# A relational message pass with one head's share on GpSimd and the one-hot tiles on VectorE

## The reference, cut to what matters

```python
# relational layer, after the attention weights alpha (one for each edge and head) are known
xl_e = xl[src, edge_type]                                   # (E, 4 heads * 128)
msg = (xl_e.reshape(E, H, C) * alpha[..., None]).reshape(E, HC)
agg = jax.ops.segment_sum(msg, seg, num_segments=N * R).reshape(N, R, H, C)
h_rel = agg.mean(axis=2) + bias                             # mean over the 4 heads
h_msg = jnp.einsum('r,nrc->nc', gw, h_rel)                  # weighted sum over the 4 relations
h1 = _layernorm(h + h_msg, g1, bt1)                         # and so on: feed-forward, layer norm
```

## Time and profile before

| | us |
|---|---|
| median of 3 runs | 8074.86 (8072.14 to 8080.34) |
| profiled execution | 8083.27 |
| span of its trace | 8081.4 |
| `rel_sum`'s lots in it, from 6104 to 6871 us | 767 |

### The profile page before, as it was taken

One profiled execution on the slowest core, in us unless ns is written; L12 is line 12 of the kernel. 1 busy time (PEld: TensorE's weight loads), 2 busy tenths in 40 slices (PEclk: granted clock), 3 DMA queues, 4 the chain that ended last, 5 costly groups with the idle time before them and its releaser, 6 DMA issues. The chain is left out here.

```text
span 8081.4 us, 86320 instructions
## 1 busy us (share of the span) xinstructions
PE 4591.5 (57%) x20103; PEld 3072.2 (38%) x20222; DVE 4954.4 (61%) x18680; ACT 1892.6 (23%) x4901; POOL 5452.5 (67%) x5731
## 2 busy tenths in 40 slices
PE   3343452444443444459788888878884566433343
PEld 3333332444433444434333333333334556333333
DVE  4333362444453444477688888888888998533334
ACT  0000031222222222231023323222235665400001
POOL 7777717777737777712277777777765777577775
PEclk6555565555565555579899999999998999655555
DMA  2111113333322333338899999999986887111111
GB/s 73 51 51 51 51 25 83 78 78 77 77 61 71 77 79 78 74 134 336 307 347 348 349 349 346 345 348 344 346 311 222 281 279 253 35 51 51 51 51 52
DMA packets 572435, 1348.04 MB, mean 167 GB/s; under 512 B 101141, under 2 KB 138997, under 8 KB 558761
## 3 DMA queue, kind: packets, MB, share of 16 engines
q0 software_dynamic: 228864, 628.13, 26.0%
q1 hardware_dynamic: 328604, 689.76, 24.1%
q10 hardware_dynamic: 14476, 24.62, 1.0%
HBM read 1003.21 MB, written 338.89 MB: 166 GB/s over the span
## 5 line engine op out<-in xcount | busy, mean ns | idle before, releaser
L942 POOL DMA_INDIRECT gat_ring<-gat_table,psrc_idx x1664 | 1643.5, 988 | 777.3 <-issue 498.2
L578 DVE TENSOR_TENSOR acc<-acc,bank 128x129 f32 (+1 forms) x1664 | 480.2, 289 | 1250.1 <-PE bank L541 1205.4
L1931 POOL DMA_INDIRECT pair<-right_table,idx_r_idx x782 | 788.5, 1008 | 365.8 <-issue 212.8
L510 POOL DMA_INDIRECT gcn_sum_ring<-gcn_table,src_idx x782 | 769.8, 984 | 275.2 <-issue 238.0
L1931 POOL DMA_INDIRECT acc<-left_table,idx_l_idx x782 | 789.9, 1010 | 238.7 <-issue 208.1
L510 POOL DMA_INDIRECT gin_sum_ring<-in_x,src_idx x782 | 781.2, 999 | 250.7 <-issue 237.1
L2006 ACT ACTIVATE positive<-positive 128x512 f32<-128x512 f32 x782 | 492.2, 630 | 1588.9 <-DVE positive L2036 1588.9
L1984 PE MATMUL bank<-pair,ident 128*128 128x512 f32 x1564 | 832.7, 615 | 1.3 <-issue 0.7
L1006 PE MATMUL bank<-gat_ring,gat_hot 128*128 128x130 f32 x3328 | 719.8, 392 | 118.1 <-DVE gat_hot L1126 116.1
L541 PE MATMUL bank<-gcn_sum_ring,gcn_sum_hot 128*128 x1664 | 417.8, 431 | 619.1 <-DMA gcn_sum_ring<-gcn_table,src_idx 586.4
L541 PE MATMUL bank<-gin_sum_ring,gin_sum_hot 128*128 x1664 | 405.2, 420 | 569.7 <-DMA gin_sum_ring<-in_x,src_idx 534.2
(11 more groups left out here) (521 smaller groups left out, 8770.9 us busy)
## 6 DMA issues: line engine op xcount, KB each, us to landing
kept<-acc SPq DMA_DIRECT2D x391, 512.0 KB, 6.1
x_rows<-kept SPq DMA_DIRECT2D x195, 1024.0 KB, 5.3
gat_place<-local_rows SPq DMA_DIRECT2D x128, 416.0 KB, 3.9
left_table<-rel_out SPq DMA_DIRECT2D x49, 1032.0 KB, 5.0
right_table<-rel_out SPq DMA_DIRECT2D x49, 1032.0 KB, 3.9
feat<-attr_rows SPq DMA_DIRECT2D x194, 256.0 KB, 7.9
gat_ring<-gat_table,psrc_idx POOLq DMA_INDIRECT x1664
types<-type_rows SPq DMA_DIRECT2D x98, 256.0 KB, 6.1
```

Of the source, the lines that this page charges most:

```text
L510: e.indirect_dma_start(ring[:, at:at + F], None, table[:, :], bass.IndirectOffsetOnAxis(ap=ed["src"][:, i:i + 1], axis=0)).then_inc(*got[b ...
L942: e.indirect_dma_start(ring[:, at:at + TROW], None, table[:, :], bass.IndirectOffsetOnAxis(ap=ed["psrc"][:, i:i + 1], axis=0)).then_inc(*g ...
L1931: e.indirect_dma_start(to[j % NG][:, n * LROW:(n + 1) * LROW], None, tab[:, :], bass.IndirectOffsetOnAxis(ap=idx[:, i:i + 1], axis=0)).the ...
```

## The change

GpSimd no longer makes one-hot tiles. For each lot it makes the product of head 2 and the weights, for the lot's four tiles in one instruction of 128 x 512, into `temper` (the tile `soft_far`, one buffer), and adds that to the four tiles' halves j = 1 with a second instruction of 128 x 512, once ScalarE has signalled `scaled`. It signals `pooled` (a semaphore whose name in the listings is `summed`; `tempered` is `relued`). VectorE keeps head 0, so 4 products for a lot where there were 8, and makes the one-hot tiles of the lot in one comparison of 128 x 512. The node numbers for it are copied once into a PSUM bank. SyncE's loads, ScalarE's copy of a new group's weights and TensorE's matmuls wait for `pooled` as well as for `mixed`. ScalarE's work is the same.

```diff
             @block.gpsimd
             def _(e):
-                e.wait_ge(*placed.at(1))
-                for i in range(LOTS):
-                    if i >= NH:
-                        e.wait_ge(*product.at(i - NH + 1))
-                    for n in range(Q):
-                        m = e.tensor_scalar(hot[i % NH][:, n * P:(n + 1) * P], c["node_iota"][:, :],
-                                            ed["local"][:, i * Q + n:i * Q + n + 1], None, ALU.is_equal)
-                    m.then_inc(*hot_made.up())
+                for b in range(FULL):
+                    g, where = group_of(b * Q)
+                    if where == 0 or b == 0:
+                        e.wait_ge(*placed.at(g + 1))
+                    e.wait_ge(*kept_in[b % NR].at(b // NR + 1, 16))
+                    if b:
+                        e.wait_ge(*pooled.at(b))
+                    n = size(b)
+                    e.tensor_tensor(temper[:, 0:n, :], lot_of(b)[:, 0:n, 2 * F:3 * F],
+                                    weights_of(b, 2).to_broadcast([P, n, F]), ALU.mult).then_inc(*tempered.up())
+                    e.wait_ge(*scaled.at(b + 1))
+                    e.wait_ge(*tempered.at(b + 1))
+                    into = parts_of(b, 1)
+                    e.tensor_tensor(into, into, temper[:, 0:n, :], ALU.add).then_inc(*pooled.up())
...
             def _(e):
                 for b in range(FULL):
                     if b >= NR:
                         e.wait_ge(*mixed.at(b - NR + 1))
+                        e.wait_ge(*pooled.at(b - NR + 1))
...
                         if g:
                             e.wait_ge(*mixed.at(b - TURN // Q))
+                            e.wait_ge(*pooled.at(b - TURN // Q))
                         put(g + 1)
...
                     e.wait_ge(*hot_made.at(b + 1))
                     e.wait_ge(*mixed.at(min(b + 1, FULL)))
+                    e.wait_ge(*pooled.at(min(b + 1, FULL)))
...
                 e.wait_ge(*placed.at(1))
+                e.tensor_copy(iota, c["node_iota"][:, :]).then_inc(*iota_laid.up())
+                e.wait_ge(*iota_laid.at(1))
...
                     if i < LOTS:
-                        g, where = group_of(i * Q)
-                        if where == FIX and g + 1 < SGROUPS:
-                            soft.mend_group_vector(e, g + 1, fixed)
+                        if i >= NH:
+                            e.wait_ge(*product.at(i - NH + 1))
+                        e.tensor_tensor(
+                            hot[i % NH][:, 0:Q * P].rearrange("p (t n) -> p t n", n=P),
+                            iota.unsqueeze(1).to_broadcast([P, Q, P]),
+                            over(ed["local"][:, i * Q:(i + 1) * Q], P), ALU.is_equal).then_inc(*hot_made.up())
                     if i < FULL:
...
                         for t_ in range(i * Q, i * Q + size(i)):
-                            for j in range(2):
-                                h = 2 * j
-                                m = e.scalar_tensor_tensor(
-                                    out=part_of(t_, j), in0=row_of(t_)[:, h * F:(h + 1) * F], scalar=weight_of(t_, h),
-                                    in1=part_of(t_, j), op0=ALU.mult, op1=ALU.add)
+                            m = e.scalar_tensor_tensor(
+                                out=part_of(t_, 0), in0=row_of(t_)[:, 0:F], scalar=weight_of(t_, 0),
+                                in1=part_of(t_, 0), op0=ALU.mult, op1=ALU.add)
                         m.then_inc(*mixed.up())
```

More of the change, by code:

```diff
@@ L2071, in rel_sum @@
             "hot_made", "scaled", "mixed", "product", "added", "fixed", "turned", "placed")
+        pooled, tempered = k.begin("summed", "relued")
+        temper = soft.far[:, 0:Q * F].rearrange("p (n f) -> p n f", f=F)
         filled, brow_made, chained, x_back = k.begin("filled", "biased", "dve", "x_loaded")
+        iota, (iota_laid,) = k.psum[BANK_V][:, 0:P], k.begin("carried")
         LAST = SCHUNKS - 1
@@ L2078, in rel_sum, with weights_of @@
         part_of = lambda i, j: weighted[:, (i % RT * 2 + j) * F:(i % RT * 2 + j + 1) * F]
+        lot_of = lambda b: x_rows[:, b % NR * Q * LROW:(b % NR + 1) * Q * LROW].rearrange("p (n f) -> p n f", f=LROW)
+        parts_of = lambda b, j: weighted[:, b * Q % RT * 2 * F:(b * Q % RT + size(b)) * 2 * F].rearrange(
+            "p (n j f) -> p n j f", j=2, f=F)[:, :, j, :]
+        def weights_of(b, h):
+            g, m = group_of(b * Q)
+            n, m = divmod(m, SPAN)
+            return weight[g % 2][:, :].rearrange("p (j q) -> p j q", q=P)[:, 0:size(b), n * 32 + h * NRUN + m // RUN].unsqueeze(2)
         def weight_of(i, h):
@@ L2108, in _ @@
                 e.wait_ge(*mixed.at(FULL))
+                e.wait_ge(*pooled.at(FULL))
                 e.dma_start(x_rows[:, :], x_kept[:, :]).then_inc(*x_back.up(16))
@@ L2138, in _ @@
                     for i in range(b * Q, b * Q + size(b)):
-                        for j in range(2):
-                            h = 2 * j + 1
+                        for j, h in enumerate((1, 3)):
                             m = e.mul(part_of(i, j), row_of(i)[:, h * F:(h + 1) * F], weight_of(i, h))
@@ L2188, in _ @@
                 e.wait_ge(*placed.at(1))
+                e.tensor_copy(iota, c["node_iota"][:, :]).then_inc(*iota_laid.up())
+                e.wait_ge(*iota_laid.at(1))
                 for i in range(LOTS + 1):
+                    g, where = group_of(i * Q)
+                    if i < LOTS and where == FIX and g + 1 < SGROUPS:
+                        soft.mend_group_vector(e, g + 1, fixed)
                     if i < LOTS:
-                        g, where = group_of(i * Q)
-                        if where == FIX and g + 1 < SGROUPS:
-                            soft.mend_group_vector(e, g + 1, fixed)
+                        if i >= NH:
[4 more added lines that the diff above has]
+                            over(ed["local"][:, i * Q:(i + 1) * Q], P), ALU.is_equal).then_inc(*hot_made.up())
                     if i < FULL:
```

## The result

The changed kernel takes 8104.06 us (median of 7 runs, 8092.09 to 8110.16) against 8072.14 (7 runs, 8060.33 to 8080.34): ratio 1.0038, 95% interval 1.0026 to 1.0049. It is slower by 0.4%, 32 us where 66 had been forecast against the same median (63 against the traces). The profiled execution took 8107.66 us, its span 8105.8. The time lies inside the stated range, the sign is right, and the size is half of what was said.

What follows compares the result with a forecast made beforehand. VectorE was taken to bind the stage, level with the load ring; lots going from 3.755 to 4.1 us gave +68 us, the last 12 lots -5, so +63 on the median 8074.9: 8138 us, range 8010 to 8215.

Steps and rivals of the forecast that it cites:

- What bounds the stage: In `rel_sum`, VectorE's own work (3 x 3.40 us) binds, level with the ring of three loads (10.2 us).
- the loop of two lots: Landing, GpSimd's product of lot b+3, VectorE's remaining products of lot b+2: (5.4 + 1.3 + 1.1) / 2 = 3.9 us a lot.
- the ring: Experiments' rival: lots are longer because of the loads' ring of three and the added waits for `pooled`; no chance given.
- The hold: VectorE's products with two SBUF inputs are blocked while GpSimd runs a 128 x 512 instruction: 1.0 us a lot.
- Mending and unevenness: In the lots, mending of scores adds 0.15 us as before and about 0.05 for meeting GpSimd; late loads add nothing.
- The last 12 lots: After the last products, VectorE's 1.84 us a lot replaces 2.3: 24.5 us instead of 29.2, -5 us.
- Gained or lost in the span, one for one: Engines leave the stage together, so what the lots gain or lose passes fully into the whole span.
- Cover holds: Rival: the block is short or falls in VectorE's additions and comparison; 3.35 us a lot, -84 us, 7991 us; chance 0.24.
- Both instructions hit: Rival: GpSimd's addition and next product both hold VectorE's products, 1.4 us on average; 4.48 a lot, +137 us, 8212; chance 0.17.
- the times above keep the two apart: Argument against two holds in a lot: by the calculated times GpSimd's addition and next product don't both meet VectorE's products.

Runs made afterwards that it cites:

- e1: Changed kernel with GpSimd's product and addition cut from 128 x 512 to 128 x 8, all waits kept; ratio 0.9861 to the kernel before, 3.27 us a lot.
- e2: Changed kernel with ScalarE writing head 1 into PSUM, so VectorE's products have one SBUF input; ratio 0.9896 to the kernel before, 3.43 us a lot.
- e3: Changed kernel with one more wait: GpSimd's product starts only after VectorE mixed the lot before; ratio 0.9979 to the kernel before, 3.77 us a lot.
- e4: Kernel before with VectorE's one-hot comparison alone, its eight products kept, GpSimd idle in the stage; ratio 1.0054 to the kernel before, 4.06 us a lot.
- e8: e2 with VectorE's comparison made one lot earlier; ratio 0.9905 to the kernel before, last 12 lots 25.2 us.
- e7: The kernel before, unchanged, traced once more; 3.733 us a lot, stage 760.8 us, rest of the span 7318.9 us.
- e13: Changed kernel plus one GpSimd comparison with a per-partition number into a spare tile; single run 8123.6 us, beside 8072.9 for the kernel before.
- e6: Changed kernel with GpSimd's addition cut to 128 x 8, its product kept at 128 x 512; ratio 0.9963 to the kernel before, 3.74 us a lot.
- e5: Changed kernel with GpSimd's product cut to 128 x 8, the full-size addition adding the half to itself; ratio 0.9943 to the kernel before, 3.58 us a lot.

## Why the prediction was half right

**What bounds the stage, and the form of the loop: right.** VectorE stays the bound, and the loop of two lots (landing, GpSimd's product of lot b+3, the rest of VectorE's products of lot b+2) is in the rows after. e1, e2 and e3 leave no room for the ring alone.

**The hold: right in kind, 0.82 instead of 1.0 us.** Two lengths were taken too large. GpSimd's product over the strided rows took 1.06 and 1.10 us in the median with either group of weights, not the 1.27 of the earlier trace rows; the addition did take 1.27. And the comparison advances VectorE by 0.60 us, not 0.68, as e4 isolates. By start-to-start steps the sum is 1.16 + 0.60 + 1.05 + 0.82 = 3.63, and the rows show 3.63 to 3.69 where 3.9 was said. That the mean over all lots is 0.83 too is in part luck: it is made of lots with no hold, with one and with two.

**Mending and unevenness: too small.** Mending's own hold is 0.09 us a lot, not 0.05, and 0.1 us is left over for late loads and changes of group, where I had added nothing. With 3.66, 0.15, 0.09 and 0.1 the lot is 4.00. The errors cancel in part: 4.00 for 4.1, which is 48 us for 68.

**The last 12 lots: wrong, -0.3 instead of -5 us.** I let VectorE's 1.84 us bind (12 lots at 0.46 less give 23.7 us, not the 24.5 of the sum). The comparison of a lot stands behind the additions of the lot before last, so TensorE gets its one-hot tiles too late and the two take turns. The chain of waits of those rows was not followed in the prediction; e8 confirms it with 25.2 us.

**"Gained or lost in the span, one for one": the step that failed.** Stage +47.4 us (by e7's trace of before 51.7), whole +32 by the medians. So 15 to 20 us, by the two traces of before 23 and 26, came back in layers that the diff doesn't touch. The stretches of gathers account for 13 us of it, 25.6 saved in the first two layers and 12.6 given back in the third and the last; one comparison more undoes this in e13. The rest stays open. No row of before could have shown that GpSimd's comparisons touch them. With the stage's true +47 alone the forecast would have been high by a third; this term, put at nothing, makes the measured change half of it.

**The rivals.** "Cover holds" needed a hold below 0.5 us and had 0.82; its numbers (3.35 a lot, -84 us) are what e1 and e2 gave once the hold was taken away: 3.27 and 3.43, -0.0139 and -0.0104 of 8066, that is -112 and -84 us, of which 17 and 19 lie outside the stage. "Both instructions hit" came about in 41 of the 196 lots, the lot at 6428.80 among them. Their second hold, 0.80 us by the means, is some 33 of the 51 us that the addition costs by e6 (0.26 a lot). Two of its steps are in that lot: one product slips between the two holds (0.34 us), and the rest wait a second time. Its mean of 1.4 us for all lots wasn't reached. "Against: the times above keep the two apart" held for quiet lots only.

## What to carry to other kernels

Before work is moved to GpSimd, list the VectorE instructions with two SBUF inputs that will run beside it (here four products took 1.87 to 1.99 us beside a GpSimd product of 1.05 to 1.15, and 1.05 without it), look at the longest of the others (L1885 has one such input and took up to 1.39 us, median 0.49), and ask when in its lot each engine starts. If they meet, try VectorE with one operand in PSUM (e2, four products in 1.11 us beside GpSimd, -1.4% against the changed kernel) before thinking of waits (e3, -0.6%). A held instruction counts as busy (a product up to 1.46 us, median 0.34), so look at the longest against the median of one line, and at start-to-start steps, not at waits or busy shares.

## What was not expected of the hardware

- GpSimd's comparisons hardly hold: beside four of 128 x 128 (0.67 us each) eight products took 2.32 us against 2.18, while one 128 x 512 instruction of 1.05 us took 0.82 us from four products. Whether their length makes the difference or their operation, which has one tensor as input, was not tested.
- VectorE's L1885, with one tensor and one number per partition from SBUF, took up to 1.39 us beside GpSimd's 128 x 512 instructions, median 0.49.
- GpSimd's product with a weight repeated along the inner axis and rows 516 numbers apart took 1.05 us at 128 x 512, less than the addition of the same size (1.27). With one tensor for both inputs the addition took 1.04 (e5).
- One GpSimd comparison with a per-partition number, in the third layer's sum, moves the median gather from 944 or 945 to 952 ns in the first two layers, and from 954 to 947 and from 952 to 945 in the third and the last.
